# Window attention and a mixture of experts on one core: four turns of the attention output stand behind the turns of the probabilities of two pairs later, and each division waits for the turn before it

## The chip, the core and the metric

The kernel runs on one core of a Trainium2 chip. The metric is the device time of one launch in microseconds (us); less is better. The core's engines run in parallel and are kept in step by semaphores: TensorE (PE in the profile, its weight loads PEld), VectorE (DVE), ScalarE (ACT), GpSimd (POOL) and SyncE (SP, which issues the DMAs). Each engine works through its own list of instructions in order.

## The reference

```python
x = x + conv(_ln_c(x))                 # x: (32, 56, 56, 96), float32
t = t + ffn(_ln_t(t))                  # t: the same values as tokens
# conv: rolled windows of 7x7 tokens, 12 heads of 8 channels
qkv = xw @ w_qkv.T + b_qkv
attn = q @ k.T / sqrt(8) + bias + mask # 49 x 49 per window and head
p = softmax(attn, axis=-1)
o = p @ v
return o @ w_proj.T + b_proj
# ffn: 4 experts, 96 -> 384 -> 96, the two best weighted by their router probabilities
h = gelu(t @ w1[e] + b1[e]);  y = h @ w2[e] + b2[e]
out = sum over e of masked[e] * y
```

## The kernel before, in words

One image is cut into four strips of 7 image columns x 56 rows, twice (two windows wide), so a unit of work is 784 tokens, 16 windows of 49 tokens. There are 32 x 4 = 128 units. The order of the work is written out by hand for each engine; the engines meet only at semaphores.

In a step of the loop three units are in work: f (its experts), a (its attention) and b (its q, k, v). TensorE's step first makes the hidden layer of f (`hidden`), then runs `attention(a, b, f)`. That has a loop over the 8 pairs of windows, n = 0 to 7. Round n of it is, in the order of TensorE's list:

- for n = 0 two groups of expert products of f (`experts`)
- `scores(a, n + 1)`: the scores of the next pair, after VectorE has read those of pair n out of the same bank
- `attend(a, n - 1)`: probabilities times values of the pair before, 24 small matmuls into bank 4 (`ps_o`); it waits until ScalarE has saved the turned probabilities, and until the division of the pair before that one is done (`onorm_done`)
- `transpose_p(a, n)`: six float32 transposes that turn the probabilities of pair n, after ScalarE's exponential
- in round 4 `transpose1(b)`, seven float32 transposes
- one more group of experts of f (two tables set which round has one; rounds 4 and 7 have none)
- `turn_o(a, n - 1)`: one float32 transpose that turns the divided attention output of pair n - 1 to channels x tokens, also into bank 4

VectorE's round n is: the gating of one or more expert results (`combine`), `softmax_pair(n + 1)` (a maximum over the scores, line 735, and a subtraction, line 739), `normalise_o(n - 1)`, and then some work for the next units (statistics, the low parts of x). The division of `normalise_o` has two instructions: a reciprocal of the row sums, which `attend` leaves in bank 4 beside the output (line 746), and a product (line 750) that writes `o_tok`, a buffer with two slots. ScalarE's round copies the turned probabilities out of PSUM (line 563), takes the exponential of the next pair (line 558) and rounds hidden activations of f.

ScalarE copies the turned outputs out of bank 4 twice per unit (`save_o`, line 574): after turn 3 and after turn 7.

In what follows, turn n is `turn_o(a, n)`, division n is `normalise_o(a, n)`, and a transpose of pair n is one of the six of `transpose_p(a, n)`.

Of the kernel before, what the change touches and what calls it, by code (L numbers as in the profile page):

```python
# [56 lines left out]
def at(unit, per_unit, k=0):  # L57

    m, c = unit
    return m * (UPI * per_unit) + (c * per_unit + k)  # L60


def first(unit):

    return isinstance(unit[0], int) and unit == (0, 0)
# [44 lines left out]


T1_AT = 4
X1_LOW_AT = ((), (), (), (), (), (0, 1), (2, 3), ())

Y_BANK = (5, 7, 6, 5, 7, 6, 7, 7, 7, 4, 7, 4)
# [2 lines left out]
N_T1, N_QK, N_V, N_S, N_PT, N_O, N_OT = 2, 4, 2, 8, 16, 8, 2  # L118
# [20 lines left out]
def build(nc, x, packed, wp, consts, out, keys):  # L139
    ctx = ExitStack()  # L140
    with ctx:
# [3 lines left out]
        def sem(name):  # L145
            return ctx.enter_context(nc.semaphore(name))
# [102 lines left out]
        onorm_done, turn_done = sem("onorm_done"), sem("turn_done")  # L249
# [379 lines left out]
        def _(dve):  # L629
# [80 lines left out]
            def x1_low(a, parts=range(4)):  # L710

                dst, hi = windows(x1_lo[0:C, :]), windows(x1_hi[0:C, :])
                for k, (j0, n) in enumerate(((0, 4), (4, 3))):
                    src = bank[5 + k][0:C, 0:n * LANES].rearrange("p (j h w r) -> p h j w r", h=2, w=NW, r=W)
                    for half in range(2):
                        if 2 * k + half not in parts:
                            continue
                        dve.wait_ge(x1hi_done, at(a, N_XHI, 2 * k + 2))
                        V.tensor_tensor(dst[:, half, :, j0:j0 + n, :].rearrange("p w j r -> p j w r"),
                                        src[:, half],  # L720
                                        hi[:, half, :, j0:j0 + n, :].rearrange("p w j r -> p j w r"),
                                        ALU.subtract).then_inc(x1lo_done, 1)
# [20 lines left out]
            def normalise_o(a, n):  # L743

                dve.wait_ge(o_done, at(a, N_O, n + 1))
                V.reciprocal(s_rec[:, :], o_heads[:, :, HD]).then_inc(rec_done, 1)
                dve.wait_ge(rec_done, at(a, N_O, n + 1))
                if n >= 2 or not first(a):
                    dve.wait_ge(turn_done, at(a, N_O, n - 1))
                V.tensor_tensor(o_tok[:, n % 2, :].rearrange("p (h d) -> p h d", d=HD), o_heads[:, :, 0:HD],  # L750
                                s_rec[:, :].unsqueeze(2).broadcast_to([SPAN, HEADS, HD]), ALU.mult
                                ).then_inc(onorm_done, 1)
# [154 lines left out]
            def attention(a, b, f=None):  # L907

                c = b and following(b)
                for n in range(8):  # L910
# [13 lines left out]
                    if b is not None:  # L924
                        x1_low(b, X1_LOW_AT[n])
                    if c is not None:
# [32 lines left out]
        def _(pe):  # L959
# [71 lines left out]
            def transpose_p(a, n):  # L1031
                if n == 0:
                    pe.wait_ge(v_saved, at(a, N_XV, N_XV))
                pe.wait_ge(exp_done, at(a, N_S, n + 1))
                for p in range(PAIRS):
                    ins = T.transpose(bank[2 + p // 4][0:SPAN, (p % 4) * 128:(p % 4) * 128 + SPAN],  # L1036
                                      p_sb[0:SPAN, n % 2, 2 * p:2 * p + 2, :].rearrange("p h k -> p (h k)")[:, 0:SPAN],
                                      ident[0:SPAN, 0:SPAN])
                    if p in (3, 5):
                        ins.then_inc(pt_done, 1)  # L1040

            def attend(a, n):

                half, wr = n // 4, 2 * (n % 4)
                pe.wait_ge(pt_saved, at(a, N_S, n + 1))
                if n:
                    pe.wait_ge(onorm_done, at(a, N_O, n))
                if n == 4:
                    pe.wait_ge(o_saved, at(a, N_OT, 1))
                for p in range(PAIRS):  # L1050
                    for s in range(2):
                        win = half * NW + wr + s
                        ins = T.matmul(ps_o[NB * s:NB * s + WW, O0 + p * 2 * VW:O0 + (p + 1) * 2 * VW],  # L1053
                                       pt_sb[0:SPAN, p, s * WW:(s + 1) * WW], v_bd[0:SPAN, win * PAIRS + p, :],
                                       start=True, stop=True, skip_group_check=True)
                ins.then_inc(o_done, 1)

            def turn_o(a, n):

                pe.wait_ge(onorm_done, at(a, N_O, n + 1))  # L1060
                o0 = (n % 4) * OTW
                T.transpose(ps_o[0:C, o0:o0 + SPAN], o_tok[:, n % 2, :], turn[:, :]).then_inc(turn_done, 1)  # L1062
# [20 lines left out]
            def gate_scores(f):  # L1083
                pe.wait_ge(x2lo_done, at(f, 2, 2))
                for j in range(W):
                    cols = slice(j * LANES, j * LANES + 128)
                    ins = three(bank[0][:, j * EXPERTS:(j + 1) * EXPERTS], x2_hi[:, cols],
                                x2_lo[:, cols], wg_hi[:, :], wg_lo[:, :])
                ins.then_inc(gate_done, 1)
# [13 lines left out]
            def experts(f, g):  # L1103

                e, j0, n = tiles_of(g)
                if e == 0:
                    pe.wait_ge(lo_dve, at(f, CPE, CPE))
                else:
                    pe.wait_ge(lo_done, at(f, N_LO, CPE * e))
                if g < 3:  # L1110
                    pe.wait_ge(gelu_done, at(f, N_H, N_H - 2 + g))
                earlier = [i for i in range(g) if Y_BANK[i] == Y_BANK[g]]
                if earlier:
                    pe.wait_ge(gated, at(f, N_Y, max(earlier) + 1))
                y = y_bank(g)[:, 0:n * C]
                T.matmul(y, ones16[:, :], b2_16[:, e * 3 * C:e * 3 * C + n * C], start=True, stop=False,
                         skip_group_check=True)
                for k in range(n):
                    cols = slice((j0 + k) * LANES, (j0 + k) * LANES + 128)
                    for c in range(CPE):  # L1120
                        slot, wc = e % 2 * CPE + c, slice((e * CPE + c) * C, (e * CPE + c + 1) * C)
                        outp = y[:, k * C:(k + 1) * C]
                        T.matmul(outp, g_hi[:, slot, cols], w2_hi[:, wc], start=False, stop=False,  # L1123
                                 skip_group_check=True)
                        T.matmul(outp, g_hi[:, slot, cols], w2_lo[:, wc], start=False, stop=False,  # L1125
                                 skip_group_check=True)
                        ins = T.matmul(outp, g_lo[:, slot, cols], w2_hi[:, wc], start=False,  # L1127
                                       stop=(c == CPE - 1), skip_group_check=True)
                ins.then_inc(y_done, 1)
# [11 lines left out]
            def attention(a, b, f=None):  # L1141


                for n in range(8):
                    groups = list(GROUPS_AT[n]) if f is not None else []
                    if n == 0 and groups:
                        experts(f, groups.pop(0))
                        experts(f, groups.pop(0))
                    if n < 7:
                        scores(a, n + 1)  # L1150
                    if n:
                        attend(a, n - 1)
                    if n == 7 and b is not None:
                        qk(b, 0)
                    transpose_p(a, n)
                    if n == T1_AT and b is not None:
                        if f is not None:

                            pe.wait_ge(gated, at(f, N_Y, 6))
                        transpose1(b)  # L1160
                    for g in groups:
                        experts(f, g)
                    if n:
                        turn_o(a, n - 1)
                if b is not None:
                    qk(b, 1)
                attend(a, 7)
                if b is not None:
                    values(b)
                turn_o(a, 7)  # L1170
                if b is not None:
                    qk(b, 2)
                project(a)
                if f is not None:
                    for g in LATE_GROUPS:
                        experts(f, g)
                transpose2(a, b)
                hidden(a, (0,))
                if f is not None:

                    pe.wait_ge(gated, at(f, N_Y, 11))
                hidden(a, (1,))
                gate_scores(a)
# [90 lines left out]
```

## Time and profile before

| | |
|---|---|
| median of 3 runs | 6585.76 us (6585.39 to 6585.8) |
| the profiled execution | 6582.02 us |
| its span | 6580.2 us |
| mean granted TensorE clock | 0.996 of full speed |
| TensorE busy (matmul, weight load) | 6329.5 us (96%), 5075.5 us (77%) |
| VectorE, ScalarE, GpSimd busy | 5021.6 (76%), 4719.7 (72%), 3763.3 us (57%) |

The span is the time from the first to the last instruction in the trace of one execution. The busy time of a matmul in the trace covers its way through the array, and matmuls in a row overlap, so the steps from one start to the next tell more than the durations. In a row of the timeline stand the start and the duration in us, the engine, the line of the kernel, the operation, what it writes and reads, and how many of the kind were merged; in brackets behind it how long the engine had been idle before, and what ended that.

### The profile page before, as it was taken

What the parts mean: (1) busy time and instruction counts of PE and PEld (TensorE: products, weight loads), DVE (VectorE), ACT (ScalarE), POOL (GpSimd) and SP (SyncE); (2) the same over time, 40 slices, a digit from 0 to 9 for tenths busy, and PEclk for the clock granted to TensorE, in tenths of its full rate; (3) what the DMA queues carried; (4) which work ended last, traced back from release to release, by engine and by line L of the source; (5) the groups of instructions that cost most, each with busy time, mean ns of one, the idle gap of its engine ahead of it and who ended that gap; (6) DMA issues with size and microseconds to landing.
All of it is one profiled execution on the core that took longest, in us unless ns stands there. A gap on an engine that the chain in (4) does not pass through costs nothing.

```text
span 6580.2 us, 265098 instructions
## 1 busy us (share of the span) xinstructions
PE 6329.5 (96%) x99456; PEld 5075.5 (77%) x99456; DVE 5021.6 (76%) x15655; ACT 4719.7 (72%) x9087; POOL 3763.3 (57%) x3337
## 2 busy tenths in 40 slices
PE   5999999999999999999999999999999999999997
PEld 4777777777777777777777777777777777777776
DVE  5777777777777777777777777777777777777775
ACT  3777777777777777777777777777777777777775
POOL 2565555555555565556555555555565555555555
PEclk9999999999999999999999999999999999999999
DMA  1111111111111111111111111111111111111110
GB/s 57 44 43 44 46 45 43 44 46 44 45 42 46 44 44 44 45 43 44 44 46 43 44 45 45 43 45 45 44 43 45 46 44 43 44 46 45 45 41 24
DMA packets 190611, 290.00 MB, mean 44 GB/s; under 512 B 42450, under 2 KB 151634, under 8 KB 189266
## 3 DMA queue, kind: packets, MB, share of 16 engines
q1 hardware_dynamic: 189394, 273.23, 14.4%
q8 instruction: 831, 13.62, 0.9%
q14 instruction: 386, 3.16, 0.2%
HBM read 138.18 MB, written 77.07 MB: 33 GB/s over the span
## 4 chain that ended last, share of the span: by engine, by line
PE 73%; DVE 15%; issue 5%; ACT 4%; POOL 2%; SPq 1%; DVEq 0%; DMA 0%; ACTq 0%; POOLq 0%
PE ps_t L1036 10%; PE ps_o L1053 9%; PE ps_f L964 8%; PE ps_f L965 8%; PE ps_f L966 8%; PE ps_s L1016 5%; PE ps_s L1026 4%; PE ps_f L1127 3%; PE ps_f L1125 3%; PE ps_f L1123 3%; DVE s_max L735 3%; PE ps_o L1062 3%; POOL rstd L437 2%; DVE stat L766 2%; PE ps_t L983 2%
## 5 line engine op out<-in xcount | busy, mean ns | idle before, releaser
L448 POOL TENSOR_TENSOR g_lo<-g_sb,g_hi 128x784 f16<-128x784 f32 x1152 | 2014.9, 1758 | 1774.3 <-DVE g_hi L873 1013.8
L541 ACT ACTIVATE g_sb<-ps_f 128x392 f32<-128x392 f32 x3072 | 1525.9, 497 | 127.6 <-PE ps_f L966 126.8
L563 ACT ACTIVATE pt_sb<-ps_t 113x588 f32<-113x588 f32 x1024 | 677.4, 662 | 1077.8 <-PE ps_t L1036 1065.0
L735 DVE TENSOR_REDUCE s_max<-ps_s 113x12 f32<-113x588 f32 x1024 | 789.1, 771 | 746.9 <-PE ps_s L1026 746.9
L1127 PE MATMUL ps_f<-w_hi,g_lo 128*128 128x96 f16 x8832 | 1227.3, 206 | 0.0
L1125 PE MATMUL ps_f<-w_lo,g_hi 128*128 128x96 f16 x8832 | 1226.7, 206 | 0.0
L1123 PE MATMUL ps_f<-w_hi,g_hi 128*128 128x96 f16 x8832 | 1226.1, 206 | 0.0
L458 POOL TENSOR_TENSOR xr<-y_gated,xr 112x192 f32<-112x192 f32 (+1 forms) x1536 | 987.0, 660 | 374.6 <-DVE y_gated L891 275.7
L964 PE MATMUL ps_f<-x_hi,w_hi 128*128 128x392 f16 x3072 | 1012.2, 329 | 19.5 <-issue 5.3
L965 PE MATMUL ps_f<-x_lo,w_hi 128*128 128x392 f16 x3072 | 1010.7, 329 | 0.0
L966 PE MATMUL ps_f<-x_hi,w_lo 128*128 128x392 f16 x3072 | 1010.6, 329 | 0.0
L1036 PE MATMUL ps_t<-ident,p_sb 113*113 113x113 f32 x6144 | 854.6, 275 | 26.9 <-ACT p_sb L558 26.7
L1125 PEld LDWEIGHTS ps_f<-w_lo,g_hi 128*128 128x128 f16 x8832 | 862.9, 98 | 10.2
L1123 PEld LDWEIGHTS ps_f<-w_hi,g_hi 128*128 128x128 f16 x8832 | 865.2, 98 | 0.1
L1127 PEld LDWEIGHTS ps_f<-w_hi,g_lo 128*128 128x128 f16 x8832 | 863.5, 98 | 0.0
L739 DVE TENSOR_TENSOR s_sub<-ps_s,s_max 113x588 f32<-113x588 f32 x1024 | 790.0, 772 | 57.0
L1053 PEld LDWEIGHTS ps_o<-v_bd,pt_sb 113*49 113x49 f32 x24576 | 738.0, 125 | 114.1 <-ACT pt_sb L563 67.1
L1053 PE MATMUL ps_o<-v_bd,pt_sb 113*49 113x18 f32 x24576 | 785.5, 198 | 24.2 <-ACT pt_sb L563 20.2
L558 ACT ACTIVATE p_sb<-s_sub 113x588 f32<-113x588 f32 x1024 | 715.7, 699 | 77.6 <-DVE s_sub L739 72.6
L1036 PEld LDWEIGHTS ps_t<-ident,p_sb 113*113 113x113 f32 x6144 | 695.9, 178 | 80.4 <-issue 51.3
L534 ACT ACTIVATE g_hi<-g_sb 128x784 f16<-128x784 f32 x768 | 647.3, 843 | 3.1 <-PE ps_f L1127 3.1
L437 POOL TENSOR_TENSOR rstd<-ve,cst 112x4 f32<-112x4 f32 (+1 forms) x256 | 270.9, 1058 | 595.4 <-DVE ve L775 595.4
(132 smaller groups left out, 13415.6 us busy)
## 6 DMA issues: line engine op xcount, KB each, us to landing
k_bd<-keys SPq DMA_DIRECT2D x1536, 36.8 KB
q_st<-qk_hi SPq DMA_DIRECT2D x768, 49.0 KB, 1.9
xr<-x SPq DMA_DIRECT2D x224, 139.1 KB
out<-xr SPq DMA_DIRECT2D x224, 139.1 KB
xa<-x SPq DMA_DIRECT2D x224, 136.5 KB
keys<-qk_hi SPq DMA_DIRECT2D x128, 147.0 KB, 2.4
keys<-qk_lo SPq DMA_DIRECT2D x128, 147.0 KB, 2.8
q_st<-qk_lo SPq DMA_DIRECT2D x384, 49.0 KB, 2.0
```

What stands on the lines that cost most here:

```text
L448: nc.gpsimd.tensor_tensor(g_lo[:, slot, 0:TOK], g_sb[:, chunk, :], g_hi[:, slot, 0:TOK], ALU.subtract).then_inc(lo_done, 1)
L458: nc.gpsimd.tensor_tensor(slot, y_gated[:, g % 4, 0:n * C], slot, ALU.add).then_inc(comb_done, 1)
L541: nc.scalar.activation(g_sb[:, chunk, half * STRIP:(half + 1) * STRIP], h_bank[k % 3][:, 0:STRIP], ACT.Gelu, scale=1.0 / WSCALE).then_inc( ...
L735: V.tensor_reduce(s_max[:, :], scores, AX.X, ALU.max).then_inc(max_done, 1)
L964: T.matmul(outp, lhs_hi, rhs_hi, start=start, stop=False, skip_group_check=True)
L965: T.matmul(outp, lhs_hi, rhs_lo, start=False, stop=False, skip_group_check=True)
L966: return T.matmul(outp, lhs_lo, rhs_hi, start=False, stop=True, skip_group_check=True)
L1036: ins = T.transpose(bank[2 + p // 4][0:SPAN, (p % 4) * 128:(p % 4) * 128 + SPAN], p_sb[0:SPAN, n % 2, 2 * p:2 * p + 2, :].rearrange("p h k ...
L1053: ins = T.matmul(ps_o[NB * s:NB * s + WW, O0 + p * 2 * VW:O0 + (p + 1) * 2 * VW], pt_sb[0:SPAN, p, s * WW:(s + 1) * WW], v_bd[0:SPAN, win ...
L1123: T.matmul(outp, g_hi[:, slot, cols], w2_hi[:, wc], start=False, stop=False, skip_group_check=True)
L1125: T.matmul(outp, g_hi[:, slot, cols], w2_lo[:, wc], start=False, stop=False, skip_group_check=True)
L1127: ins = T.matmul(outp, g_lo[:, slot, cols], w2_hi[:, wc], start=False, stop=(c == CPE - 1), skip_group_check=True)
```

## The change

Two tables now say in which round which turn stands, and where in the round: turns 0, 1, 2 and 4 move from the end of rounds 1, 2, 3 and 5 to the place right behind the transposes of rounds 2, 3, 4 and 6. Turns 3, 5, 6 and 7 stay where they were. On VectorE the wait for a turn moves from the product to the reciprocal, and it is a later turn: division n waited for turn n - 2 (the slot of `o_tok` that it writes), and now waits for turn n - 1.

```diff
 T1_AT = 4
+TURNS_BEHIND_P = ((), (), (0,), (1,), (2,), (), (4,), ())
+TURNS_AT_END = ((), (), (), (), (3,), (), (5,), (6,))
...
             def normalise_o(a, n):
 
                 dve.wait_ge(o_done, at(a, N_O, n + 1))
+                if n or not first(a):
+                    dve.wait_ge(turn_done, at(a, N_O, n))
                 V.reciprocal(s_rec[:, :], o_heads[:, :, HD]).then_inc(rec_done, 1)
                 dve.wait_ge(rec_done, at(a, N_O, n + 1))
-                if n >= 2 or not first(a):
-                    dve.wait_ge(turn_done, at(a, N_O, n - 1))
...
                     transpose_p(a, n)
+                    for m in TURNS_BEHIND_P[n]:
+                        turn_o(a, m)
                     if n == T1_AT and b is not None:
...
                     for g in groups:
                         experts(f, g)
-                    if n:
-                        turn_o(a, n - 1)
+                    for m in TURNS_AT_END[n]:
+                        turn_o(a, m)
```

TensorE's list at the end of round 1 of a unit, before: the last products of an expert group (`w_hi`, `w_lo` are the second expert weights, `g_hi`, `g_lo` the hidden activations in two halves), turn 0, and the first scores of pair 3.

```order
L1125 MATMUL ps_f<-w_lo,g_hi 128x96
L1127 MATMUL ps_f<-w_hi,g_lo 128x96
L1062 MATMUL ps_o<-turn,o_tok 96x113 [waits onorm_done]
L1016 MATMUL ps_s<-bias,sel 64x8x49 [waits sub_done]
L1016 MATMUL ps_s<-bias,sel 49x8x49
```

The same place now (line numbers are two or more higher in the changed kernel):

```order
L1127 MATMUL ps_f<-w_lo,g_hi 128x96
L1129 MATMUL ps_f<-w_hi,g_lo 128x96
L1018 MATMUL ps_s<-bias,sel 64x8x49 [waits sub_done]
L1018 MATMUL ps_s<-bias,sel 49x8x49
L1022 MATMUL ps_s<-ul,selB 49x8x49
```

The scores follow the experts directly; turn 0, with its wait for the division, is gone from here.

TensorE's list in the middle of round 2, before: the output of pair 1, the six transposes of pair 2, and the first products of the next expert group.

```order
L1053 MATMUL ps_o<-v_bd,pt_sb 49x18 [waits onorm_done,pt_saved]
L1053 MATMUL ps_o<-v_bd,pt_sb 49x18 x11
L1036 MATMUL ps_t<-ident,p_sb 113x113 [waits exp_done]
L1036 MATMUL ps_t<-ident,p_sb 113x113 x5
L1116 MATMUL ps_f<-b_16,ones 128x192 [waits gated,lo_done]
L1123 MATMUL ps_f<-w_hi,g_hi 128x96
```

The same place now:

```order
L1055 MATMUL ps_o<-v_bd,pt_sb 49x18 [waits onorm_done,pt_saved]
L1055 MATMUL ps_o<-v_bd,pt_sb 49x18 x11
L1038 MATMUL ps_t<-ident,p_sb 113x113 [waits exp_done]
L1038 MATMUL ps_t<-ident,p_sb 113x113 x5
L1064 MATMUL ps_o<-turn,o_tok 96x113 [waits onorm_done]
L1118 MATMUL ps_f<-b_16,ones 128x192 [waits gated,lo_done]
```

Turn 0 stands between the transposes and the experts, as a seventh float32 transpose. In round 4 the place behind the transposes is in front of `transpose1(b)`, which is float32 too.

VectorE's list in round 2, before: the softmax of pair 3, the division of pair 1 and the first statistics.

```order
L735 TENSOR_REDUCE s_max<-ps_s 113x12 [waits s_done]
L739 TENSOR_TENSOR s_sub<-ps_s,s_max 113x12x49 [waits exp_done,max_done]
L746 RECIPROCAL s_rec<-ps_o 113x12 [waits o_done]
L750 TENSOR_TENSOR o_tok<-ps_o,s_rec 113x96 [waits turn_done,rec_done]
L697 BN_STATS stat<-xa 112x6 x2
```

The same place now:

```order
L737 TENSOR_REDUCE s_max<-ps_s 113x12 [waits s_done]
L741 TENSOR_TENSOR s_sub<-ps_s,s_max 113x12x49 [waits exp_done,max_done]
L750 RECIPROCAL s_rec<-ps_o 113x12 [waits turn_done,o_done]
L752 TENSOR_TENSOR o_tok<-ps_o,s_rec 113x96 [waits rec_done]
L699 BN_STATS stat<-xa 112x6 x2
```

The wait for a turn now stands in front of both instructions of the division, and it is for the turn of the same round.

## Rows read from the trace of the kernel before

**Rows 1.** The page's first line.
```profile
span 6580.2 us, 265098 instructions
```

**Rows 2.** Waits over the whole span: us in total, times, longest us.
```profile
PEld ps_o L1062 <- DVE o_tok L750: 50.3, 133, 1.0
```

**Rows 3.** Timeline, TensorE from experts to scores without a turn (end of round 0).
```profile
3009.96 0.21 PE L1127 MATMUL ps_f<-w_hi,g_lo 128*128 128x96 f16 x1
...
3010.10 0.36 PE L1016 MATMUL ps_s<-bias,sel 128*64 128x392 f16 x2
```

**Rows 4.** Timeline, TensorE and VectorE around turn 0 (end of round 1).
```profile
3012.60 0.26 DVE L750 TENSOR_TENSOR o_tok<-ps_o,s_rec 113x96 f32<-113x96 f32 x1
...
3012.74 0.21 PE L1127 MATMUL ps_f<-w_hi,g_lo 128*128 128x96 f16 x1
...
3012.91 0.30 PE L1062 MATMUL ps_o<-turn,o_tok 113*96 113x113 f32 x1
...
3013.14 0.36 PE L1016 MATMUL ps_s<-bias,sel 128*64 128x392 f16 x2
```

**Rows 5.** Timeline, TensorE around turn 1 (end of round 2).
```profile
3016.04 0.21 PE L1127 MATMUL ps_f<-w_hi,g_lo 128*128 128x96 f16 x1
...
3016.43 0.36 PE L1016 MATMUL ps_s<-bias,sel 128*64 128x392 f16 x2
```

**Rows 6.** Timeline, TensorE around turn 2 (end of round 3).
```profile
3019.50 0.21 PE L1127 MATMUL ps_f<-w_hi,g_lo 128*128 128x96 f16 x1
...
3019.54 0.27 PE L1062 MATMUL ps_o<-turn,o_tok 113*96 113x113 f32 x1
...
3019.74 0.36 PE L1016 MATMUL ps_s<-bias,sel 128*64 128x392 f16 x2
```

**Rows 7.** Timeline, TensorE around turn 4 (end of round 5).
```profile
3025.66 0.21 PE L1127 MATMUL ps_f<-w_hi,g_lo 128*128 128x96 f16 x1
...
3025.90 0.36 PE L1016 MATMUL ps_s<-bias,sel 128*64 128x392 f16 x2
```

**Rows 8.** Timeline, TensorE in round 7: six transposes, turn 6, qk.
```profile
3030.38 0.76 PE L1036 MATMUL ps_t<-ident,p_sb 113*113 113x113 f32 x6
...
3030.98 0.26 PE L1062 MATMUL ps_o<-turn,o_tok 113*96 113x113 f32 x1
...
3031.07 0.33 PE L964 MATMUL ps_s<-x_hi,wqk_hi 128*96 128x392 f16 x1
```

**Rows 9.** Timeline of round 4: transposes, their copy, division 3, turn 3.
```profile
3020.89 0.85 PE L1036 MATMUL ps_t<-ident,p_sb 113*113 113x113 f32 x6
...
3021.58 0.83 PE L972 MATMUL ps_f<-ident,xn 112*96 112x112 f32 x7
3021.78 0.66 ACT L563 ACTIVATE pt_sb<-ps_t 113x588 f32<-113x588 f32 x1 [1.32 <-PE ps_t L1036]
...
3021.98 0.22 DVE L746 RECIPROCAL s_rec<-ps_o 113x12 f32<-113x12 f32 x1
...
3022.54 0.12 PEld L1062 LDWEIGHTS ps_o<-turn,o_tok 113*96 113x96 f32 x1 [0.36 <-DVE o_tok L750]
```

**Rows 10.** Timeline of round 6: first expert after the transposes, division 5, turn 5.
```profile
3027.99 0.25 PE L1116 MATMUL ps_f<-b,ones 128*128 128x192 f16 x1
...
3028.39 0.22 DVE L746 RECIPROCAL s_rec<-ps_o 113x12 f32<-113x12 f32 x1
...
3028.80 0.21 PE L1127 MATMUL ps_f<-w_hi,g_lo 128*128 128x96 f16 x1
...
3028.95 0.30 PE L1062 MATMUL ps_o<-turn,o_tok 113*96 113x113 f32 x1
```

**Rows 11.** Timeline, VectorE's idle time before the maxima of rounds 2 and 3.
```profile
3014.14 0.77 DVE L735 TENSOR_REDUCE s_max<-ps_s 113x12 f32<-113x588 f32 x1 [0.53 <-PE ps_s L1026]
...
3017.18 0.77 DVE L735 TENSOR_REDUCE s_max<-ps_s 113x12 f32<-113x588 f32 x1 [0.45 <-PE ps_s L1026]
```

**Rows 12.** All turns: count, duration ns least/median/most, first and last start.
```profile
L1062 PE MATMUL ps_o<-turn,o_tok x1024: 260/301/395, 84.7 to 6519.5; 113*96 113x113 f32 x171
```

## What it will do to the time, predicted before the run

> **What bounds the kernel now.** I read the waits first, then one unit of the timeline engine by engine, and last the steps of TensorE around each turn. The unit is one of 127 alike (units 1 to 127 have experts beside their attention; the first has none), and its times lie near 3010 us. The profiled span is 6580.2 us [rows 1].
>
> In every round VectorE ends its work, stands idle, and starts the next maximum only when TensorE's scores are there: 0.53 us idle in round 2, 0.45 in round 3 [rows 11]. So in the attention TensorE sets the pace, and what shortens its list in a round shortens the round, as long as VectorE keeps some of that idle time. There are places where it is the other way round: TensorE waits for a division before a turn, 133 times, one or so per unit [rows 2]. That row counts only idle time past the end of the matmuls in flight, so the smaller waits have to be read from start to start.
>
> From expert product to scores, with no turn between, TensorE takes 0.14 us from start to start [rows 3]. With a turn between it takes:
>
> - turn 0: 0.40 us (3012.74 to 3013.14), because the division ends at 3012.86 and the turn starts only at 3012.91, 0.17 after the product [rows 4]
> - turn 1: 0.39 us [rows 5], alike
> - turn 2: 0.24 us; this turn starts 0.04 behind the product and waits for nothing [rows 6]
> - turn 4: 0.24 us [rows 7], alike
>
> **What the change takes away.** Each of the four turns leaves its place between experts and scores. If 0.14 us is what is left there, rounds 1, 2, 3 and 5 lose 0.26, 0.25, 0.10 and 0.10 us: 0.71 us in a unit. Part of that is the turn itself, part the wait for the division (about 0.13 us each at turns 0 and 1). The scores that come forward need the scores of the round before to have been subtracted; at the end of round 1 VectorE is past that: the product of division 0, which it makes after the subtraction, starts at 3012.60 [rows 4], before TensorE is through with the experts. They don't wait for it.
>
> **What it adds on TensorE.** A turn behind transposes exists already: in round 7, six transposes take 0.60 us from their first start to the start of turn 6, 0.10 each, and the turn 0.09 to the next matmul [rows 8]. The next matmul is float16 there as it will be in rounds 2, 3 and 6. I take 0.10 us for a turn in the new place. The bounds: 0.09 below, and above it 0.23, the step from a turn that stands alone to what follows (3012.91 to 3013.14 [rows 4]). I take the lower end, since rows 8 are the same sequence of instructions.
>
> - Round 2 gets turn 0: +0.10. Round 3 gets turn 1: +0.10.
> - Round 4 gets turn 2, in front of the seven transposes of the next unit. Nothing is paid there: turn 3 at the end of that round has TensorE idle for 0.36 us until division 3 is done [rows 9], and that division hangs on the scores at the round's start, not on what TensorE does later. The 0.10 goes into that wait. With the cover gone it would cost 0.10.
> - Round 6 gets turn 4. Turn 5 at that round's end starts 0.15 us behind the last product (3028.80 to 3028.95 [rows 10]), where one that doesn't wait starts 0.04 behind it [rows 6]. So 0.11 us is wait for division 5, and 0.10 goes into it. Nothing is left of that cover, and nothing is paid.
>
> [...]
>
> **What it adds on VectorE.** Division n now waits for turn n - 1. For divisions 4, 6 and 7 that turn lies far back. For divisions 1, 2, 3 and 5 it is the one that moved, in the same round, so this is the new risk. How late does it come? The copy of the turned probabilities shows when a result behind such a stream can be used: in round 4 the six transposes start at 3020.89, 0.10 apart, so the last at 3021.48, and ScalarE starts at 3021.78, 0.30 after it [rows 9]. Turn 2 will start where the next unit's transposes do now, 3021.58, and can be used at 3021.88. Division 3 starts at 3021.98 [rows 9]. In round 6 turn 4 starts at 3027.99, where the experts do now, is of use at 3028.29, and division 5 starts at 3028.39 [rows 10]. Both start times hang on the same scores, so the 0.10 us between them stays whatever the rounds before do. Rounds 2 and 3 have the same order and the same margin. So I take no delay.
>
> The bound above: the longest turn in the trace is 395 ns, where one in a stream is 260 [rows 12, 8]; with it the division would start 0.04 late. Behind the division are queued the statistics or low parts of the next units, the gating and the next maximum; they would take a few hundredths out of idle time in rounds 2 and 3 [rows 11]. In rounds 4 and 6 turns 3 and 5 wait for the division directly, and a delay there is paid in full: 0.04 twice, 0.08 us in a unit.
>
> By the Trainium skill, Perfetto Trace Analysis, section Tensor Engine Instruction, the end of a matmul in a profile is an estimate, and the write to PSUM and the semaphore come after it. That speaks against trusting the 0.10 us, and gives no size. The trace agrees that something comes after the end shown, but the 0.30 us above are from a start to the consumer's start, and hold it.
>
> **The sum.** -0.26 - 0.25 - 0.10 - 0.10 + 0.10 + 0.10 + 0 + 0 = -0.51 us in a unit, times 127 = -65 us. The profiled span goes from 6580.2 to 6515 us; the median of the runs stands 5.6 above that span, so 6585.8 becomes 6521. VectorE keeps 0.27 us of idle time before the maximum of round 2 (0.53 - 0.26) and 0.30 in round 3 (0.45 - 0.15), so it doesn't become the bound. What comes after round 7 is neither longer nor shorter.
>
> **The rivals.**
>
> - *The turn is dear behind the transposes too.* At 0.23 us each in rounds 2 and 3, and 0.23 - 0.11 = 0.12 left in round 6, the sum is -0.71 + 0.58 = -0.13 us, -16 us in all: 6569. Against it stand rows 8. With the late divisions of 0.08 alone the sum is -0.43, 6531. Any mixture lies between.
> - *Nothing happens,* because the rounds are tied by the loop scores, subtraction, division, output, and not by TensorE's list, and the 0.51 turns into idle time before the next scores: 6586, give or take 13. For it: turns 0, 1, 3 and 5 do wait for divisions. Against it: the idle times of VectorE before each maximum [rows 11], larger than what is taken.
> - *Slower, by the new wait.* Place: divisions 3 and 5. A turn is now behind transposes that wait for ScalarE's exponential, so a late exponential delays the division, and that delays turns 3 and 5, on which the next scores wait. It decides from 0.255 us of delay in each of the two rounds (then the 0.51 is gone). At 0.31 us each the kernel is 0.11 us slower in a unit, 6600. The turn would have to be of use 0.76 us after the last transpose's start (3021.48 to 3021.98 is 0.50, and 0.255 more), where the rows give 0.40, so little speaks for it.
> - *More than the sum,* if experts and scores without a turn step at 0.04 instead of 0.14 us (the product-to-turn step of rows 6): 0.40 us more in a unit, 51 us: 6470. Rows 3 speak against it.
>
> **How the numbers follow.** A change under 0.2% (13 us) I count as the same, about what a measurement of this kernel can tell. The forecast, -45 to -75 us, 0.74; the turn dear or divisions late, 0.12 (nearly all of it still faster by over 13 us); nothing, 0.07; slower, 0.04; more than the sum, 0.03. Faster: 0.74 + 0.03 + 0.10 = 0.87, same 0.07 + 0.02 = 0.09, slower 0.04. The predicted time is 6521. The range from 6508 to 6552 holds the forecast and the half of the second case that is nearer to it, about 8 in 10; the forecast's own is 6511 to 6541.
>
> **What would show it.** In the changed profile the step from expert product to scores at the ends of rounds 1, 2, 3 and 5 should be 0.14 us; the turn behind the transposes should add 0.10 us to the experts' start; TensorE's idle time before turn 3 should be 0.26 instead of 0.36 us; turn 5 should follow its product in 0.05; VectorE's divisions should start as long after their maximum as before (a division with idle time ended by a turn would show the late-division case); and VectorE's idle time before the maximum of round 2 should be near 0.27. I am wrong if the divisions of rounds 4 and 6 start more than 0.05 us later after their maximum, or if the step from a turn to the experts is over 0.15 us.

## The result, and the profile after

The changed kernel takes 6519.99 us (median of 4 runs, 6518.15 to 6520.04), the kernel before 6585.78 (6585.39 to 6586.61). The ratio is 0.990, 95% interval 0.988 to 0.992: 66 us less, where 65 were predicted. The span of the profiled execution went from 6580.2 us [rows 1] to this (first line of the page):

```profile
span 6516.3 us, 265099 instructions
```

The rows below are from the timeline of one unit of the changed kernel, TensorE's steps at the ends of rounds 1, 2, 3 and 5: the last expert product, then the first scores.

```profile
2982.43 0.21 PE L1129 MATMUL ps_f<-w_hi,g_lo 128*128 128x96 f16 x1
2982.57 0.36 PE L1018 MATMUL ps_s<-bias,sel 128*64 128x392 f16 x2
...
2985.57 0.21 PE L1129 MATMUL ps_f<-w_hi,g_lo 128*128 128x96 f16 x1
2985.71 0.44 PE L1018 MATMUL ps_s<-bias,sel 128*64 128x392 f16 x4
...
2988.88 0.21 PE L1129 MATMUL ps_f<-w_hi,g_lo 128*128 128x96 f16 x1
2989.01 0.44 PE L1018 MATMUL ps_s<-bias,sel 128*64 128x392 f16 x4
...
2994.94 0.21 PE L1129 MATMUL ps_f<-w_hi,g_lo 128*128 128x96 f16 x1
2995.08 0.36 PE L1018 MATMUL ps_s<-bias,sel 128*64 128x392 f16 x2
```

All four steps are 0.13 to 0.14 us, where they were 0.40, 0.39, 0.24 and 0.24 [rows 4 to 7].

The same unit's round 2: the transposes, turn 0 in its new place, the first of the experts, and division 1.

```profile
2983.98 0.85 PE L1038 MATMUL ps_t<-ident,p_sb 113*113 113x113 f32 x6
2984.67 0.26 PE L1064 MATMUL ps_o<-turn,o_tok 113*96 113x113 f32 x1
2984.76 0.25 PE L1118 MATMUL ps_f<-b,ones 128*128 128x192 f16 x1
...
2985.06 0.22 DVE L750 RECIPROCAL s_rec<-ps_o 113x12 f32<-113x12 f32 x1
```

Six transposes take 0.69 us to the start of what follows, as before, and the turn 0.09 more.

Round 4: turn 2 between the transposes of pair 4 and those of the next unit, division 3, turn 3 with its wait. Then round 6: turn 4, the last expert product and turn 5.

```profile
2990.86 0.26 PE L1064 MATMUL ps_o<-turn,o_tok 113*96 113x113 f32 x1
2990.95 0.84 PE L974 MATMUL ps_f<-ident,xn 112*96 112x112 f32 x7
...
2991.26 0.22 DVE L750 RECIPROCAL s_rec<-ps_o 113x12 f32<-113x12 f32 x1
...
2991.82 0.12 PEld L1064 LDWEIGHTS ps_o<-turn,o_tok 113*96 113x96 f32 x1 [0.26 <-DVE o_tok L752]
...
2997.18 0.26 PE L1064 MATMUL ps_o<-turn,o_tok 113*96 113x113 f32 x1
...
2998.08 0.21 PE L1129 MATMUL ps_f<-w_hi,g_lo 128*128 128x96 f16 x1
2998.14 0.30 PE L1064 MATMUL ps_o<-turn,o_tok 113*96 113x113 f32 x1
```

The wait before turn 3 shrank from 0.36 [rows 9] to 0.26 us, the step from the product to turn 5 from 0.15 [rows 10] to 0.06: both moved turns fell into waits that were there.

VectorE's maxima of rounds 1 to 3, in the same unit, and over the span the waits for them and those of turns for divisions (us in total, times, longest):

```profile
2980.54 0.77 DVE L737 TENSOR_REDUCE s_max<-ps_s 113x12 f32<-113x588 f32 x1 [0.18 <-PE ps_s L1028]
...
2983.57 0.77 DVE L737 TENSOR_REDUCE s_max<-ps_s 113x12 f32<-113x588 f32 x1
...
2986.46 0.77 DVE L737 TENSOR_REDUCE s_max<-ps_s 113x12 f32<-113x588 f32 x1 [0.28 <-PE ps_s L1028]
```
```profile
DVE s_max L737 <- PE ps_s L1028: 651.6, 990, 18.6
...
PEld ps_o L1064 <- DVE o_tok L752: 36.1, 130, 0.9
```

From the maximum of round 2 to that of round 3 it is 2.89 us, where it was 3.04 [rows 11]: VectorE follows TensorE, with idle time left, as the prediction had it. In the unit shown only 0.14 us of idle time stand right before the maximum of round 2 and 0.20 before the statistics ahead of it; as the median of 126 units, the idle time before that maximum fell from 0.70 to 0.44 us.

From the first scores at the end of one round to those at the end of the next, as the median of 126 units, the rounds changed by -0.257, -0.152, -0.005, +0.002 and -0.102 us for rounds 1 to 5, and the rest of the unit by +0.003: -0.51 us in a unit, 65 us in 127.

### The profile page after: what moved, and what is told of

Its sections match the earlier page's. It is cut to its first block, busy times and chain, and to the rows that moved or that the text cites. A ratio compares the mean times of both kernels' runs of the same rounds, so it can differ in the third digit from the quotient of the medians.

```text
span 6516.3 us, 265099 instructions
## 1 busy us (share of the span) xinstructions
PE 6280.1 (96%) x99456; PEld 5077.8 (78%) x99456; DVE 5032.7 (77%) x15655; ACT 4717.1 (72%) x9087; POOL 3756.0 (58%) x3337
## 3 DMA queue, kind: packets, MB, share of 16 engines
q8 instruction: 831, 13.62, 0.9%
## 4 chain that ended last, share of the span: by engine, by line
PE 76%; DVE 13%; ACT 4%; issue 3%; POOL 2%; SPq 1%; DVEq 0%; DMA 0%; ACTq 0%; POOLq 0%
PE ps_t L1038 12%; PE ps_o L1055 10%; PE ps_f L966 8%; PE ps_f L967 8%; PE ps_f L968 8%; PE ps_s L1018 5%; PE ps_s L1028 4%; PE ps_f L1129 4%; PE ps_f L1127 4%; PE ps_f L1125 4%; POOL rstd L439 2%; PE ps_o L1064 2%; DVE stat L768 2%; PE ps_f L1070 2%; PE ps_t L985 2%
```

## The experiments

Each ran against the kernel before on the same chip (6584.7 to 6586.1 us there). The edits are to the changed kernel.

**Parts of the change.** Turns 0 and 1 alone, turns 2 and 4 alone, and the new wait alone:

```diff
 # turns 0 and 1
-TURNS_BEHIND_P = ((), (), (0,), (1,), (2,), (), (4,), ())
-TURNS_AT_END = ((), (), (), (), (3,), (), (5,), (6,))
+TURNS_BEHIND_P = ((), (), (0,), (1,), (), (), (), ())
+TURNS_AT_END = ((), (), (), (2,), (3,), (4,), (5,), (6,))
 # turns 2 and 4
+TURNS_BEHIND_P = ((), (), (), (), (2,), (), (4,), ())
+TURNS_AT_END = ((), (0,), (1,), (), (3,), (), (5,), (6,))
 # the wait alone
+TURNS_BEHIND_P = ((), (), (), (), (), (), (), ())
+TURNS_AT_END = ((), (0,), (1,), (2,), (3,), (4,), (5,), (6,))
```

> Only turns 0 and 1 stand behind the transposes of two pairs later; turns 2 and 4 are back at the end of their rounds. Theory (what is gained is waiting: turns 0 and 1 no longer wait for their divisions, and turns 2 and 4 fall into the waits before turns 3 and 5): rounds 1 and 2 lose 0.26 and 0.25 us, rounds 2 and 3 get 0.10 each, -0.31 us in a unit, -39 us, 6547. Rival (the place among float32 transposes gives the same for each turn): half of the whole gain, -33 us, with a turn 2 at the end of round 3 that costs as much as turn 0 did there. The trace parts them: by the theory the step around turn 2 stays 0.24 us.

> Only turns 2 and 4 stand behind the transposes; turns 0 and 1 are back at the ends of rounds 1 and 2. Theory (waiting): rounds 3 and 5 lose 0.10 us each, and the two turns cost nothing in rounds 4 and 6, where TensorE's idle time before turn 3 goes from 0.30 to 0.20 us behind the product and the step from the last product to turn 5 from 0.15 to 0.06: -0.20 us in a unit, -25 us, 6560. With the first run it adds up to the whole change. Rival (place): -33 us, half of the whole, and no such fall of the two waits.

> All turns at the ends of their rounds as before the change; only the wait of each division is the changed one (for the turn before it, ahead of the reciprocal). Theory: every such turn is done before the division could start, so nothing: 6586, within 3 us. Rival (the second wait in front of the reciprocal costs time to get through VectorE's queue, so that the change paid for it somewhere): each division some 0.05 us later after its maximum, and as turns 0, 1, 3 and 5 wait for it, up to 0.2 us in a unit, +25 us.

Measured: turns 0 and 1, 6543.81 us, ratio 0.994 (0.992 to 0.995), 41 us less than before. Turns 2 and 4, 6556.67 us, ratio 0.996 (0.994 to 0.997), 28 less. The wait alone, 6584.92, ratio 1.000 (0.999 to 1.001). The two parts add up to 69 us where the whole gave 66, within what the intervals can tell. The sums of waiting (39 and 25) are nearer than two equal halves (33 each), but with intervals of some 11 us to either side the times alone don't part the theories; the traces do. From scores to scores a unit is 0.31 us shorter with turns 0 and 1 alone (39 us in 127) and 0.20 with turns 2 and 4 alone (25 us), as the median of the units. Turns 0 and 1 alone, the end of round 3 (product, turn 2, scores):

```profile
3002.41 0.21 PE L1129 MATMUL ps_f<-w_hi,g_lo 128*128 128x96 f16 x1
3002.46 0.26 PE L1064 MATMUL ps_o<-turn,o_tok 113*96 113x113 f32 x1
3002.65 0.44 PE L1018 MATMUL ps_s<-bias,sel 128*64 128x392 f16 x4
```

Turn 2 in its old place takes 0.24 us, 0.10 more than no turn: as much as behind the transposes. Its move saves nothing by itself. Turns 2 and 4 alone, the ends of rounds 4 and 6:

```profile
3010.79 0.12 PEld L1064 LDWEIGHTS ps_o<-turn,o_tok 113*96 113x96 f32 x1 [0.26 <-DVE o_tok L752]
...
3017.05 0.21 PE L1129 MATMUL ps_f<-w_hi,g_lo 128*128 128x96 f16 x1
3017.11 0.30 PE L1064 MATMUL ps_o<-turn,o_tok 113*96 113x113 f32 x1
```

The waits before turns 3 and 5 shrank by 0.10 and 0.09 us. So what was gained is waiting: two waits left out, and two others filled.

**How much margin the new wait has.** One extra issue of each moved turn, in the same place:

```diff
                 o0 = (n % 4) * OTW
+                for _ in range(1 if n in (0, 1, 2, 4) else 0):
+                    T.transpose(ps_o[0:C, o0:o0 + SPAN], o_tok[:, n % 2, :], turn[:, :])
                 T.transpose(ps_o[0:C, o0:o0 + SPAN], o_tok[:, n % 2, :], turn[:, :]).then_inc(turn_done, 1)
```

> The changed kernel, and each of the four moved turns is issued twice in a row, the first without a signal (the same values to the same place). Theory: a turn behind the transposes costs 0.10 us of TensorE; rounds 2 and 3 pay it, round 4 hides it in the wait before turn 3, and in round 6 only 0.02 us of cover is left, so it pays 0.08: +0.28 us in a unit, +36 us over the changed kernel, 6556. The division's margin of 0.10 us is just used up, so the divisions move by no more than a few hundredths. Rival (the turn's signal comes close to late already): divisions 3 and 5 go 0.10 us late and are paid in full in round 4 too: +0.40 us, +51 us, 6571.

Measured: 6562.17 us, ratio 0.997 (0.995 to 0.998), 42 over the changed kernel, between the two. Round 4, the second issue of turn 2, division 3 and turn 3:

```profile
3011.62 0.26 PE L1066 MATMUL ps_o<-turn,o_tok 113*96 113x113 f32 x1
...
3011.99 0.23 DVE L750 RECIPROCAL s_rec<-ps_o 113x12 f32<-113x12 f32 x1
...
3012.57 0.12 PEld L1066 LDWEIGHTS ps_o<-turn,o_tok 113*96 113x96 f32 x1 [0.24 <-DVE o_tok L752]
```

The turn came 0.10 us later, and the division 0.06 to 0.07 later after its maximum (medians over 126 units: 1.49 us from maximum to reciprocal in the changed kernel, 1.55 to 1.56 here). So the margin was 0.03 us, not 0.10. The reciprocal starts 0.37 us after the turn, where ScalarE's copy starts 0.30 after a transpose [rows 9]. Round 4 paid 0.07 for it.

Then with the two waits of the division the other way round:

```diff
-                dve.wait_ge(o_done, at(a, N_O, n + 1))
                 if n or not first(a):
                     dve.wait_ge(turn_done, at(a, N_O, n))
+                dve.wait_ge(o_done, at(a, N_O, n + 1))
```

> The run with one extra turn, and the two waits of each division in the other order in the code: the wait for the output is now the separate one, and the reciprocal itself carries the wait for the turn (before, the other way round). In the run with one extra turn the reciprocal starts 0.37 us after the turn's start, where ScalarE's copy starts 0.30 us after the last transpose, and so divisions are 0.06 to 0.07 us late after their maximum. Theory A (the 0.07 is the way of VectorE's queue past a separate wait): the reciprocal starts 0.30 us after the turn, the divisions are late by under 0.01, round 4 pays nothing: 0.07 us in a unit less than that run, 9 us, 6553. Theory B (the signal of a turn itself takes 0.37 us): nothing changes, 6562, and divisions stay 0.06 to 0.07 us late.

Measured: 6549.45 us, ratio 0.994 (0.993 to 0.996), 13 under the run before it. The same three rows:

```profile
3004.70 0.26 PE L1066 MATMUL ps_o<-turn,o_tok 113*96 113x113 f32 x1
...
3005.00 0.23 DVE L750 RECIPROCAL s_rec<-ps_o 113x12 f32<-113x12 f32 x1
...
3005.57 0.12 PEld L1066 LDWEIGHTS ps_o<-turn,o_tok 113*96 113x96 f32 x1 [0.17 <-DVE o_tok L752]
```

The reciprocal starts 0.30 us after the turn. In the trace each reciprocal carries one wait, and the second is an instruction of its own in front of it: for the turn in the run above, for the output here. When that one is the last to end, the way from there to the start costs 0.07 us more. The other side shows it too: divisions 6 and 7, which wait for their outputs, start 0.31 us after the output's last matmul in this run and 0.25 in the run above. The Trainium skill, Perfetto Trace Analysis, section Identifying Dependency Chains, says that such waiting instructions may be put in front; it gives no price, and the 0.07 us are this run's. The four us beyond the nine expected came from round 6, where division 5 is earlier too and turn 5 no longer waits for it: from turn 5 to the output behind it the step is 0.19 us instead of 0.23.

**The price when the margin is gone.** The loop's count set to 3, for all four turns and then for turns 2 and 4 alone:

```diff
-                for _ in range(1 if n in (0, 1, 2, 4) else 0):
+                for _ in range(3 if n in (0, 1, 2, 4) else 0):
 # the second run
+                for _ in range(3 if n in (2, 4) else 0):
```

> The changed kernel with each of the four moved turns issued four times in a row, only the last with a signal: the price of the new wait once its margin is gone. The first of these runs left a margin of 0.03 us (the divisions went 0.06 to 0.07 late for 0.097 us more). Theory: each round 2 and 3 pays 0.29 us on TensorE; the divisions are 0.26 us late; in round 4 turn 3 waits for division 3 and pays 0.26; in round 6 the last product comes 0.27 us past its cover and pays that: 1.11 us in a unit, +141 us over the changed kernel, 6661, slower than before the change. Rival (a late division is hidden by VectorE's idle time in round 4 as in rounds 2 and 3): 0.85 us, +108 us, 6628.

> The changed kernel with three extra issues of turns 2 and 4 alone, the two whose divisions are waited for directly. The run with three extra issues of all four came out 155 us over its sum, with an idle time of TensorE of some 3.6 us at 30 places, once per pass of the loop; it has 48 turns more in the loop's body. Theory of the new wait: divisions 3 and 5 are 0.26 us late, round 4 pays 0.26 and round 6 0.28, 0.54 us in a unit, +69 us over the changed kernel, 6589: the point where the new wait has eaten the whole gain. With 24 turns more in the loop's body, and the run with 16 more free of the long idle times, I expect none of them. Rival (late divisions bring the long idle times): 30 of them again, 6740.

Measured: all four, 6817.24 us, ratio 1.035 (1.033 to 1.037), 156 over the expected 6661. Turns 2 and 4, 6586.92 us, ratio 1.001 (1.000 to 1.002), 2 under the expected 6589. In the second, the last of the four issues, the division, and turn 3:

```profile
3022.19 0.26 PE L1066 MATMUL ps_o<-turn,o_tok 113*96 113x113 f32 x1
...
3022.56 0.23 DVE L750 RECIPROCAL s_rec<-ps_o 113x12 f32<-113x12 f32 x1 [0.17 <-PE ps_o L1066]
...
3023.13 0.12 PEld L1066 LDWEIGHTS ps_o<-turn,o_tok 113*96 113x96 f32 x1 [0.24 <-DVE o_tok L752]
```

Now VectorE stands idle for the turn, by name, and the whole gain of the change is eaten. That is the slower rival of the prediction, brought about by extra turns: it decides at 0.26 us of delay in each of two rounds. In the first run the rounds, too, cost what was expected (0.29, 0.29, 0.27 and 0.28 us, 142 us in all). The rest is one thing that has nothing to do with divisions. Waits of the first run, a pass of the loop in its timeline, and two stretches behind it (the number after POOL's is the granted clock):

```profile
PEld ps_f L966 <- issue: 128.3, 165, 3.8
PE ps_f L966 <- issue: 101.9, 30, 3.7
```
```profile
318.29 0.16 PE L966 MATMUL ps_s<-wg_hi,x_hi 128*128 128x4 f16 x1
322.12 0.10 PEld L966 LDWEIGHTS ps_f<-x_hi,w_hi 128*128 128x128 f16 x1 [3.72 <-issue]
```
```profile
322.00:324.00 2.00, 1.87 (x6) 0.89 (x7) 0.03 (x1) 0.61 (x2) 0.00 (x0) 0.50 0.32 80
...
326.00:328.00 2.00, 2.00 (x14) 1.19 (x13) 1.94 (x4) 2.00 (x5) 0.00 (x0) 1.00 0.15 35
```

At 30 places, the passes of the loop, TensorE stands idle for over 3 us with nothing to wait for, and then runs at the lower of its two clock levels (0.50 of 2.4 GHz, 1.2) before it is back at the full one. Whether that comes with the late divisions or with the longer program was to be told by a run that is as long and lets no division wait for a turn:

```diff
+                for _ in range(12 if n == 6 else 0):
```

> The changed kernel with twelve extra issues of turn 6, which stands behind the transposes of round 7: as many more turns in the loop's body (48) as in the run with three extra issues of four turns, but no division is late by it, since division 7 starts 1.69 us after turn 6 and needs 0.37. TensorE alone pays 12 x 0.097 = 1.16 us in a unit, 148 us. Theory A (the long idle times come with the length of TensorE's program in the loop): 30 of them again, +155 us, 6823. Theory B (they come with the late divisions or the changed rounds): none, 6668.

Measured: 6773.46 us, ratio 1.029 (1.027 to 1.030). Waits of this run, and the same of the run with turns 2 and 4 alone:

```profile
PE ps_f L966 <- issue: 97.1, 30, 3.8
```
```profile
PE ps_f L966 <- issue: 5.3, 30, 0.2
```

The 30 idle times are there, and no division comes late by a turn: division 7, the only one behind the extra turns, starts 1.47 us after the last of them. Theory A holds. The sum was 50 us too high. Some 29 us of that are extra turns that fell into the wait of the output of pair 7 for ScalarE's copy (67.0 us over the span in the changed kernel, 0.5 here), so that a unit became 0.93 instead of 1.16 us longer. The other 20 are the passes, which cost 4.5 us each here and 5.2 in the first run.

**The same for turns 3 and 5.** If waiting is what was gained, the waits left are at turns 3 and 5.

```diff
-TURNS_BEHIND_P = ((), (), (0,), (1,), (2,), (), (4,), ())
-TURNS_AT_END = ((), (), (), (), (3,), (), (5,), (6,))
+TURNS_BEHIND_P = ((), (), (0,), (1,), (2,), (3,), (4,), ())
+TURNS_AT_END = ((), (), (), (), (), (), (5,), (6,))
...
-                if n == 4:
+                if n == 5:
                     pe.wait_ge(o_saved, at(a, N_OT, 1))
...
                 act.wait_ge(turn_done, at(a, N_O, 4 * half + 4))
+                if half == 0:
+                    act.wait_ge(onorm_done, at(a, N_O, 5))
...
                     copy_pt(a, n)
+                    if n == 5:
+                        save_o(a, 0)
...
                     if n == 4:
-                        save_o(a, 0)
 # the second run, besides
+TURNS_AT_END = ((), (), (), (), (), (), (), (6,))
...
                     if n:
                         attend(a, n - 1)
+                    if n == 7:
+                        turn_o(a, 5)
```

> The changed kernel with turn 3 too behind the transposes of two pairs later (round 5). The copy of the first four turns, which waited for turn 3 in round 4, moves to round 5 on ScalarE, between the copy of the turned probabilities and the exponential, and waits for division 4 too; the output of pair 5 instead of pair 4 waits for it. If the gain is waiting, the two waits left around turn 3 should come free as well: the step from the last transpose of the next unit to the scores goes from 0.53 (0.30 to the turn, 0.23 behind it) to 0.10 us, the wait of the output of pair 4 for ScalarE's copy (0.19 us) goes, and turn 3 costs 0.10 in round 5: -0.52 us in a unit, -66 us against the changed kernel, 6454. Rival (VectorE, with 0.29 us of idle time before the maximum that follows, is the bound in round 4 then): -0.29 us, -37 us, 6483.

> The same, and turn 5 stands behind the output of pair 6 in round 7 (float32 matmuls) instead of ahead of it. The output waits for division 5 as the turn did, so it starts when the turn started; the turn's 0.23 us step goes, and 0.10 us come behind the output: -0.13 us in a unit, -17 us against the run with turn 3 alone, 6437 if that gives 6454. Rival (division 6, which now waits for turn 5 behind the output, comes late and turn 6 with it): no gain over that run.

Measured: turn 3 too, 6453.98 us, ratio 0.980 (0.978 to 0.981); turns 3 and 5, 6451.24 us, ratio 0.980 (0.978 to 0.981). The first is 66 us under the changed kernel, the time expected, though the parts were not: from scores to scores round 4 lost 0.34 us where 0.43 were expected, because turn 2 had already taken 0.10 of that wait, and round 5 lost 0.14 where 0.09 were. That is 0.48 us in a unit, 61 us, so the exact agreement is partly luck. VectorE as the bound (6483) is refuted. The second gave 3 us where 17 were expected. Turn 3 too: the next unit's transposes and the first scores behind them, and the waits that are left:

```profile
2969.54 0.84 PE L977 MATMUL ps_f<-ident,xn 112*96 112x112 f32 x7
...
2970.30 0.45 PE L1021 MATMUL ps_s<-bias,sel 128*64 128x392 f16 x4
```
```profile
PEld ps_o L1067 <- DVE o_tok L755: 1.6, 2, 0.9
...
PE ps_o L1058 <- ACT o_sb L578: 0.5, 1, 0.5
```

From the first of seven transposes to the scores it is 0.76 us; nothing stands between. The waits of turns for divisions fell from 36.1 to 1.6 us, those of outputs for ScalarE's copy from 31.9 to 0.5. Round 7 in the same run, from the last expert product over turn 5 (left out) and the output of pair 6 to the next q and k:

```profile
2976.19 0.21 PE L1132 MATMUL ps_f<-w_hi,g_lo 128*128 128x96 f16 x1
...
2976.48 0.73 PE L1058 MATMUL ps_o<-v_bd,pt_sb 113*49 113x18 f32 x24
...
2977.14 0.37 PE L969 MATMUL ps_s<-x_hi,wqk_hi 128*96 128x392 f16 x1
```

With turn 5 moved too, the same place:

```profile
2968.14 0.21 PE L1132 MATMUL ps_f<-w_hi,g_lo 128*128 128x96 f16 x1
2968.28 0.73 PE L1058 MATMUL ps_o<-v_bd,pt_sb 113*49 113x18 f32 x24
2968.95 0.30 PE L1067 MATMUL ps_o<-turn,o_tok 113*96 113x113 f32 x1
2969.09 0.33 PE L969 MATMUL ps_s<-x_hi,wqk_hi 128*96 128x392 f16 x1
```

The output starts 0.14 to 0.15 us behind the product instead of 0.29, so the old place gives back 0.14 us and not 0.23. In the new one the steps on the two sides of the turn are 0.13 and 0.14 us, where the output alone had one step of 0.13: the turn costs 0.14, not 0.10. The two cancel, and from product to q and k it is 0.95 us in both runs. So the neighbours do matter: a turn costs 0.10 us behind the six transposes and 0.14 behind the 24 small matmuls of an output. The 0.04 us that the unit gained lie behind, nearly all in the step from the first matmul of q and k to the second (0.17 instead of 0.20). The rival (division 6 late) isn't needed for that; VectorE does wait for turn 5 now (58.8 us, 130 times), but turn 6 still starts 0.10 us behind the transposes, without a wait.

## Why the prediction was right, point by point

- *The four places at the ends of the rounds:* 0.14 us each remained, as taken from round 0. The 0.71 us of the sum are there, and the rival in which 0.04 remain is refuted.
- *The turn in the new place:* 0.10 us, the lower bound. The rival in which it is dear behind the transposes is refuted, for that place.
- *Turns 2 and 4 cost nothing:* they fell into the waits for divisions 3 and 5, as the two shrunken waits show, in the changed kernel and with these turns alone.
- *VectorE isn't the bound:* its steps from maximum to maximum followed TensorE's, so the rival in which nothing happens is refuted. The idle time before the maximum of round 2 fell by 0.26 us as forecast, but from 0.70 to 0.44 as a median: the 0.53 of the unit that was read, and so the 0.27, are not those of most units. The 0.30 of round 3 are 0.28.
- *No division is late:* right in its effect, but the margin was mis-sized. I took 0.10 us from ScalarE's copy; VectorE's start behind a separate wait comes 0.07 us later, so 0.03 were left. The waits of the change alone cost nothing, and the margin held; with one turn more it didn't. That nothing was paid was in part luck: 0.03 us of reserve were left, not the 0.10 that the prediction reasoned with.
- *The sum:* -65 us forecast, -64 in the profiled spans, -66 in the medians.

## What to carry to other kernels

Read the cost of an instruction that waits as a step from start to start, beside the same step without it: 0.26 us of turn 0 were 0.10 of work and 0.16 of waiting, and the waits view counted nearly none of it. An instruction whose result nobody needs yet may stand later on its engine's list, where its input has long been there, and best where it falls into a wait that another one has anyway. If a buffer forces a new wait for it, measure that wait's margin by making the awaited instruction later on purpose, before building on it.

## What the runs showed of the hardware that was not expected

- A VectorE instruction behind two waits starts 0.37 us after the start of the turn it waits for if the separate wait ends last, and 0.30 if its own does. TensorE shows the same: in the changed kernel the output of pair 4 starts 0.05 us after the end of ScalarE's copy of the turned outputs in the 124 units where the wait for that copy is the instruction's own, and 0.11 in the 4 where it is a separate instruction.
- With 48 turns more in the loop's body TensorE stands idle for 2.9 to 3.8 us at each of 30 passes, with 24 more for 0.2; a pass then costs 4.5 and 5.2 us more in the two runs, with the stretch at 1.2 GHz behind the idle time. The page of both long runs counts 860 packets and 14.09 MB on the queue of kind instruction, where all others have 831 and 13.62: 29 more, one for each of the 29 whole passes (27 instead of 26), of 16 KiB each. In both long runs, and in none of the ten other traces, such a packet falls into each of the 30 idle times: it starts 0.2 to 1.0 us after TensorE has fallen idle and takes 1.0 us (median), and TensorE goes on 2.6 to 3.2 us after its start. By the Trainium skill, Runtime: NRT & Kernel Launch, section Instruction fetch mechanics, an engine fetches its program in blocks of 16 KiB, and a taken branch whose target isn't at hand waits for a fetch. The trace agrees in the size and in the wait. So TensorE waits at the back edge for a block that has to be fetched. It wasn't tried apart from the length, and where the limit lies between 24 and 48 turns stays open; the shorter loops fetch 26 blocks in a pass as well, without such a wait.
